# A fused attention, recurrence and mixture-of-experts kernel: the drain of its second phase in another written order, with a second buffer for the expert output

## The reference, cut to what matters

```python
x = x + _layernorm(attention(_layernorm(x)))        # 16 heads
x = x + _layernorm(fp8_gemm(_layernorm(x)))
x = x + _layernorm(hawk_block(_layernorm(x)))       # conv, gates, scan, gated MLP
x = x + _layernorm(mixture(_layernorm(x)))
```

## Time and profile before

| what | value |
|---|---|
| median of 3 runs | 1355.8 us |
| lowest, highest | 1354.93, 1356.39 us |
| profiled execution, its own time | 1354.26 us |
| its span from first to last instruction | 1352.5 us |
| mean granted TensorE clock | 0.957 |
| busy: PE, DVE, ACT, POOL | 1199.3 (89%), 1119.7 (83%), 974.4 (72%), 808.0 (60%) us |

### The profile page before, as it was taken

One profiled execution on the slowest core, in us unless ns is written; L12 is line 12 of the kernel. 1 busy time (PEld: TensorE's weight loads), 2 busy tenths in 40 slices (PEclk: granted clock), 3 DMA queues, 4 the chain that ended last, 5 costly groups with the idle time before them and its releaser, 6 DMA issues.

```text
span 1352.5 us, 26168 instructions
## 1 busy us (share of the span) xinstructions
PE 1199.3 (89%) x8688; PEld 497.3 (37%) x8688; DVE 1119.7 (83%) x2357; ACT 974.4 (72%) x1780; POOL 808.0 (60%) x1091
## 2 busy tenths in 40 slices
PE   1789999999999999999999999977979999999863
PEld 0223233333332333333333332333545555655442
DVE  2867999999999999999999899856658878878756
ACT  1267877887888787788788787777758687787640
POOL 6304447467466466466566545536878888888752
PEclk8589999999999999999999998999989999999985
DMA  1131011011011011011011010000000000000000
GB/s 50 52 88 43 27 45 42 28 44 41 29 44 39 31 43 40 31 43 39 32 43 33 29 36 12 2 1 1 1 8 9 9 16 8 9 17 9 16 9 24
DMA packets 52517, 37.87 MB, mean 28 GB/s; under 512 B 8864, under 2 KB 51744, under 8 KB 52384
## 3 DMA queue, kind: packets, MB, share of 16 engines
q1 hardware_dynamic: 52384, 36.22, 8.4%
HBM read 6.31 MB, written 4.19 MB: 8 GB/s over the span
## 4 chain that ended last, share of the span: by engine, by line
PE 34%; DVE 26%; issue 15%; POOL 11%; ACT 10%; SPq 4%; DMA 0%; ACTq 0%; POOLq 0%; DVEq 0%
PE bank L201 10%; PE bank L182 9%; DVE neg_max L493 9%; PE bank_pair L169 4%; PE bank L228 3%; SPq L641 3%; PE bank L210 3%; DVE probs L1172 2%; PE bank L235 2%; ACT probs L381 2%; DVE y_q L472 1%; ACT probs L1024 1%; POOL x_all L1491 1%; DVE probs L1348 1%; DVE probs L1344 1%
## 5 line engine op out<-in xcount | busy, mean ns | idle before, releaser
L381 ACT ACTIVATE probs<-bank 128x512 f32<-128x512 f32 x1024 | 569.4, 599 | 165.6 <-PE bank L182 163.1
L493 DVE TENSOR_REDUCE neg_max<-bank_pair 128x2 f32<-128x1024 f32 x512 | 610.3, 1214 | 88.4 <-PE bank_pair L169 86.2
L182 PE MATMUL bank<-q_stack,k_stack 50*128 50x512 bf16 x1024 | 352.3, 388 | 31.3 <-ACT probs L381 22.9
L201 PE MATMUL bank<-probs,v_pad 128*32 128x256 f32 x4096 | 331.9, 394 | 0.4 <-issue 0.2
L169 PE MATMUL bank_pair<-k_stack,q_stack 48*128 48x512 bf16 x1024 | 292.3, 395 | 33.5 <-DMA k_stack<-k_parts 18.0
L182 PEld LDWEIGHTS bank<-q_stack,k_stack 50*128 50x128 bf16 x1024 | 79.3, 93 | 275.6 <-ACT probs L381 234.2
L201 PEld LDWEIGHTS bank<-probs,v_pad 128*32 128x32 f32 x4096 | 83.0, 108 | 166.8 <-issue 160.3
L794 PE MATMUL bank_pair<-probs,w_gates 128*128 128x512 f32 x256 | 118.7, 607 | 5.8 <-DVE probs L1641 2.9
L567 POOL TENSOR_SCALAR tiny<-mv_b 128x4 f32<-128x4 f32 x16 | 4.0, 250 | 146.9 <-DVE mv_b L52 146.9
L522 POOL TENSOR_TENSOR q_rest<-q_rest,q_parts 128x512 f32<-128x512 f32 x16 | 20.2, 1260 | 119.7 <-ACT q_rest L325 119.7
L169 PEld LDWEIGHTS bank_pair<-k_stack,q_stack 48*128 48x128 bf16 x1024 | 53.9, 94 | 58.7 <-DVE neg_max L493 37.0
(11 more groups left out here) (249 smaller groups left out, 2250.2 us busy)
## 6 DMA issues: line engine op xcount, KB each, us to landing
q_stack<-q_parts SPq DMA_DIRECT2D x384, 32.0 KB
k_stack<-k_parts SPq DMA_DIRECT2D x384, 32.0 KB
x_all<-in_z_dram SPq DMA_DIRECT2D x16, 256.0 KB, 3.0
out_dram<-x_all SPq DMA_DIRECT2D x16, 256.0 KB, 2.3
q_stack<-max_rows SPq DMA_DIRECT2D x64, 8.0 KB
w_gates<-in_w_gates_dram SPq DMA_DIRECT2D x1, 512.0 KB, 3.8
w_in<-in_w_in_dram SPq DMA_DIRECT2D x1, 256.0 KB, 2.9
w_grow<-in_w_grow_dram SPq DMA_DIRECT2D x1, 256.0 KB, 4.0
```

Of the source, the lines that this page charges most:

```text
L182: nc.tensor.matmul(st_ps[h][:, :], k_stack[par][rows, p, c * P:(c + 1) * P], q_stack[par][rows, p, :], start=True, stop=True).then_inc(s[" ...
L201: mm = nc.tensor.matmul(acc[32 * g:32 * g + 32, cols], v_pad[bpar][:, kc, 4 * a + g, :], probs[:, at + g, cols], start=(t == 0 and kc == 0 ...
L381: nc.scalar.activation(probs[:, 4 * (n % RING) + g, :], st_ps[g % 2][:, :], ACT.Exp, scale=SCALE)\
L493: nc.vector.tensor_reduce(neg_max[j // 4][:, c, j % 4, :], score_ps[c % 2][:, :, :], AX_X, ALU.max, negate=True).then_inc(s["max_read"], 1)
```

## The change

In the drain only. PE: `gate_in(NB)` ahead of `cumulated(NB)`. ACT: `decay(NB)` ahead of `route_exps(NB)`. DVE: `routed_out(NB+1)` moves behind `ranks(NB+2)`, and `norm_x3(NB+2)` from behind `exps_inv(NB+2)` to ahead of `ranks(NB+2)`; the last batch's counts are neither summed nor added; its two instructions for the largest logit go ahead of the bias sum, and its mean and variance behind `exps_inv`. POOL: `root_x3(NB+2)` ahead of `routed_root(NB+1)`. The expert output of iteration NB+2 is written to `acc_y`, with statistics of its own. In the loop the written instructions are the same as before.

```diff
@@ tensor, drain
             forget(NB)
+            gate_in(NB)
             cumulated(NB)
-            gate_in(NB)
             wout(NB)
@@ scalar, drain
+            decay(NB)
             route_exps(NB)
-            decay(NB)
             square(NB)
@@ vector
+        def y_of(i):
+            return (acc_y, "y_odd") if i == NB + 2 else (y, "y")
+        def largest(i):
...
+        def below_largest(i):
...
+        def stats_y(i):
+            if live(i, -4):
+                aggregate(y_of(i)[1], "y", i - 4)
         def routed(i):
...
+                y, which = y_of(i)
                 wait(dve, s["y_ps"], b + 1)
+                if i > NB + 2:
+                    largest(i)
+                    below_largest(i)
                 if i > NB + 1:
-                    wait(dve, s["x4_ready"], b)
+                    wait(dve, s["x4_ready"], b - 1)
                 else:
                     wait(dve, s["yc_ready"], b)
                 TT(y..., bank_y..., consts["b_expert"]..., ALU.add).then_inc(s["y_ready"], 1)
+                if i <= NB + 2:
+                    largest(i)
                 wait(dve, s["y_ready"], b + 1)
-                raw("y", "y", chunk(y))
...
+                raw(which, "y", chunk(y))
+                if i <= NB + 2:
+                    below_largest(i)
+                    stats_y(i)
@@ place_sum
-                wait(dve, s["count_step"], 2 * b + 1)
-                TT(counts[:, :], counts[:, :], counted[:, :], ALU.add).then_inc(s["count_step"], 1)
+                if b < NB - 1:
+                    wait(dve, s["count_step"], 2 * b + 1)
+                    TT(counts[:, :], counts[:, :], counted[:, :], ALU.add).then_inc(s["count_step"], 1)
@@ vector, drain
             norm_t(NB + 2)
-            routed_out(NB + 1)
             raw_x3(NB + 2)
             stats_x3(NB + 2)
             routed(NB + 2)
+            norm_x3(NB + 2)
             ranks(NB + 2)
+            routed_out(NB + 1)
             exps_sum(NB + 2)
             exps_inv(NB + 2)
-            norm_x3(NB + 2)
             counts_of(NB + 2)
...
             exps_inv(NB + 3)
-            counts_of(NB + 3)
+            stats_y(NB + 3)
             place(NB + 3)
@@ pool, drain
             x3_sum(NB + 2)
+            root_x3(NB + 2)
             routed_root(NB + 1)
             routed_sum(NB + 1)
-            root_x3(NB + 2)
             routed_root(NB + 2)
```

More of the change, by code:

```diff
@@ L705, in hawk_moe_phase @@
     xc_pad = padded[:, 0:T + TAPS - 1]
-    stats = {n: (sb(f"bn_{n}", [P, C, 6]), sb(f"mv_{n}", [P, C, 2])) for n in ("t", "x3", "y")}
+    stats = {n: (sb(f"bn_{n}", [P, C, 6]), sb(f"mv_{n}", [P, C, 2])) for n in ("t", "x3", "y", "y_odd")}
     h_sum = sb("h_sum", [P, C])
@@ L1185, in taps @@
                     conv[par][:, 1, :], ALU.mult, ALU.add).then_inc(q, 1)
+        def y_of(i):
+            return (acc_y, "y_odd") if i == NB + 2 else (y, "y")
+        def largest(i):
+            b, q = i - 4, s["top_step"]
+            wait(dve, s["logits_ps"], b + 1)
+            nc.vector.tensor_reduce(top[:, 0, :], log_ps.rearrange("p (c e) -> p c e", e=E), AX_X, ALU.max)\
+                .then_inc(q, 1)
+        def below_largest(i):
+            b, q = i - 4, s["top_step"]
+            wait(dve, q, 2 * b + 1)
+            wait(dve, s["route_step"], 5 * b)
+            wait(dve, s["exps_ready"], b)
+            TT(shifted[:, :, :], log_ps.rearrange("p (c e) -> p c e", e=E),
+               top[:, 0, :].unsqueeze(2).to_broadcast([P, C, E]), ALU.subtract).then_inc(q, 1)
+        def stats_y(i):
+            if live(i, -4):
+                aggregate(y_of(i)[1], "y", i - 4)
         def routed(i):
@@ L1196, in routed @@
                    consts["b_expert"][:, :].unsqueeze(1).to_broadcast([P, C, D]), ALU.add).then_inc(s["y_ready"], 1)
[L1197 to L1200, removed]
+                if i <= NB + 2:
+                    largest(i)
                 wait(dve, s["y_ready"], b + 1)
-                raw("y", "y", chunk(y))
[L1203 to L1208, removed]
+                raw(which, "y", chunk(y))
+                if i <= NB + 2:
+                    below_largest(i)
+                    stats_y(i)
         def routed_out(i):
             b = i - 4
+            y, which = y_of(i)
             wait(dve, s["rs_y_step"], 5 * (b + 1))
-            scaled(y, chunk(y), stats["y"][1], rs["y"][:, 2, :], s["yn_part"])
+            scaled(y, chunk(y), stats[which][1], rs["y"][:, 2, :], s["yn_part"])
             wait(dve, s["yn_part"], C * (i - NB))
@@ L1508, in routed_root @@
                 wait_apart(gp, s["stat_y"], C * (b + 1), past_wait)
-                TT(top[:, 5, :], top[:, 4, :], stats["y"][1][:, :, 1], ALU.mult).then_inc(q, 1)
+                var = stats["y_odd" if i == NB + 2 else "y"][1][:, :, 1]
+                TT(top[:, 5, :], top[:, 4, :], var, ALU.mult).then_inc(q, 1)
                 wait_apart(gp, q, at + 2, past_wait)
```

## The result

| | before | changed |
|---|---|---|
| median, us (10 runs each) | 1354.66 | 1347.29 |
| lowest to highest | 1350.48 to 1356.63 | 1344.52 to 1350.92 |
| ratio of the two, 95% interval | | 0.9946 [0.9933, 0.9959] |
| span of the profiled execution | 1352.5 | 1343.6 |

The changed kernel is 7.4 us (0.54%) faster by medians, 5.5 to 9.1 by the interval. The forecast was 1349.9 with a range of 1346.5 to 1352.8.

The account below looks back on a forecast made before the run. The prediction took the drain to be bound by late gate_in(NB) on PE and norm_x3(NB+2) on DVE. Gains 2.2 + 3.2 = 5.4 from a mean of 1355.35 gave 1349.9, range 1346.5 to 1352.8.

Parts of the forecast that it names:

- the two places: In the drain's chain: gate_in(NB) on PE at 1280.92, 5.06 us, and norm_x3(NB+2) on DVE at 1335.34.
- The gates on PE and ACT: gate_in(NB) follows forget without pause at full clock; ACT reaches its tanh pair L1057 at 1281.37, 4.64 earlier.
- Exclusion between VectorE and GpSimd: Around the scans of iteration NB, wide instructions exclude each other, leaving 2.2 of 4.64; L1477 starts at 1292.0.
- The clock: On PE from wout(NB+1) onward: chain as before, only 2.2 earlier, so no gain or loss from clock in the sum.
- rival (c): PE from 1301.0 to 1322.3: a fifth to a quarter at half speed, losing about 3, giving 1352.9; chance 0.14.
- part 1: Last gates: gate_in(NB) ahead of cumulated(NB) on PE, decay(NB) ahead of route_exps(NB) on ACT; gain 2.2 us.
- The last batches: End of drain: norm_x3(NB+2) and routed_out(NB+1) reordered, second buffer; last logits at 1335.1 instead of 1338.30, gain 3.2.
- Inner order and counts of the last batch: Last batch on DVE: 5.21 from y stays within 0.2, and the counts left out gain nothing.
- ACT's half of part 1: On ACT, decay(NB) no longer waits for shifted and starts at 1277.69 instead of 1279.14; no separate gain given.
- rival (a): DVE and POOL collide not at all or more cheaply: gains 6.6 to 7.8, 1347.6 at the far end; chance 0.22.
- its own signs: Things to see in the profile, among them the last batch's bias sum L1195 near 1336.7 with both gains.
- Rival (d): PE's clock stays at 1.2 GHz through 1301.0 to 1322.3: slower than before, 1357.8; chance 0.05.

Follow-up runs that it names:

- Small_pool: Changed kernel with GpSimd's three wide instructions of iteration NB cut from 512 to 4 elements a partition; 1348.61 us, ratio 0.9951.
- no_act: Changed kernel with ACT's old order, route_exps(NB) ahead of decay(NB); 1348.33 us over 12 runs, ratio 0.9948.
- pe_only: Kernel before with only PE's gate_in(NB) moved ahead of cumulated(NB), ACT as before; 1351.28 us, ratio 0.9973.
- p1_only: Kernel before with only gate_in(NB) ahead of cumulated(NB) on PE and decay(NB) ahead of route_exps(NB) on ACT; 1353.26 us, ratio 0.9985.
- pool_late: Changed kernel with GpSimd's mixture work of iteration NB moved later, whole, behind norm_h(NB) to x3_sum(NB) and further steps; 1351.27 us, ratio 0.9968.
- after_again: Changed kernel measured a second time, no edit, against the kernel before; 1348.84 us against 1354.74, ratio 0.9959.
- pool_fit: Changed kernel with GpSimd's mixture work of iteration NB moved into gaps away from VectorE's L1172 groups; 1345.52 us (7 runs), ratio 0.9942.
- p2_only: Changed kernel with both PE's and ACT's reorderings of the gates undone; 1349.42 us, ratio 0.9963.
- one_buffer: Changed kernel with a single buffer y, routed_out(NB+1) ahead of routed(NB+2), root_x3(NB+2) behind routed_sum(NB+1); one run, 1349.68 us.

## Why the prediction was right, point by point

The forecast named the two places, the new wait in each and the sign of every term of its sum. Against the profile of the changed kernel:

- **The gates on PE and ACT.** Forecast 4.64 earlier for the tanh pair; measured 8.71 - 3.98 = 4.73. No pause on PE, and ACT sets the moment and not PE, if only by 0.08: both as said.
- **Exclusion between VectorE and GpSimd.** Forecast as the reason why only 2.2 of 4.64 arrive; measured 2.69, since the collisions cost 2.04 and not 2.4. The order of events is the one that was played through: L1541 waits for L1325, L1479 for L1367, the first scan for L1479, L1495 for the first scan, L1497 for the second. Small_pool shows that it is GpSimd's wide work: without it 2.06 comes back. The rule of the Trainium skill (page "SBUF — State Buffer", section "SBUF: two separate sides") gave the right reading for the wide instructions; by a sum without it the drain would have been 2 us shorter than it was. For GpSimd's small power instruction the whole-instruction lock does not fit the trace (last section), and there the measurement decides; the forecast had taken its length from the rows.
- **The clock.** This term was missing from the sum. The forecast took `wout(NB+1)` and the growth products as unchanged; in the changed kernel's profile the third stretch is 0.92 shorter (11.07 against 11.99), because the clock returned sooner (0.56 in `wout(NB+1)` and 0.40 in the growth products, less 0.04 elsewhere). The clock stood in the range and in rival (c), with the sign the other way. And `gate_in` after its pause, taken as 5.06, is 6.6 in another profile, so part 1's gain was undersized for some executions.
- **The last batches.** Forecast 3.2, measured 23.02 - 19.58 = 3.44. The logits are released by `placed` as said. Of the two edits that bring them forward, `norm_x3`'s place is worth 2.56, the second buffer with `routed_out`'s place 1.6 (not additive: each alone leaves the transposes late). `routed_out(NB+2)` and the last y did tie, with no wait added.
- **Inner order and counts of the last batch, GpSimd's root.** Forecast nothing, 0.06 and 0.12 measured. ACT's half of part 1 was not priced by itself. Up to `norm_h(NB)` it costs 0.34 (no_act) to 0.53 (pe_only against p1_only), since it moves VectorE into GpSimd's way; over the whole drain the profiles do not settle its sign.
- **The sum.** 2.69 + 0.92 + 3.44 = 7.05 in the drain, against 5.4. The mis-sized terms are the clock (0.9), the collisions (0.4), the gates (0.1) and the last batches (0.2). Of the 2.6 between 1349.9 and 1347.29, another 0.7 is the level of the kernel before, 1354.66 over ten runs and not 1355.35.
- **Luck, and the scatter.** The measured 1347.29 lies nearer to rival (a)'s 1347.6 than to the forecast, and yet (a), the rival without collisions, did not happen: the scans took 3.28, and L1500 (L1477 before) came 14.18 into the drain, where (a) needed 12.3. The time was inside the range by a margin that was put there for another mechanism and for scatter; the timeline, and not the time, shows that the forecast's mechanism is the one. The scatter itself was taken as 0.16% from four values; ten runs of the kernel before spread over 0.45%. By the second set of runs, 0.41%, the forecast of 0.40% looks exact, which is chance as well. Of its own signs, one missed: the last bias sum starts at 1333.59 + 1.84 = 1335.43 in the old profile's times, 1.3 ahead of the 1336.7 forecast.

Rival (d), the clock at 1.2 GHz through 1301 to 1322, did not show in any of the 14 profiles: the fourth stretch, which covers most of it, is 19.99 to 20.01 in all but pool_late.

Open stays how much of the gain by time is the clock. In the drain it is 0.92 of 7.05 in the first profile and 0.55 of 6.68 in after_again. The third stretch is 11.32 us on average in the seven profiles in which GpSimd is held up (10.20 in the second stretch), and 11.95 in the six, pool_fit aside (its centring adds 0.67 there), in which the stretch ahead of it is short (8.14 to 8.34). Taking GpSimd's delay away thus seems to bring the low clock into `wout`, and to give back a part of the gain, but with a spread of up to 1.25 within a group that is a tendency and not a price. Nor does PE's idle time ahead of it settle it: the kernel before, p2_only and pool_fit all had 5.73 us of it, and their `wout` took 3.75, 3.14 and 3.05.

## What to carry to other kernels

When an instruction off the critical path is moved into another engine's idle time, ask who used that idle time: the gates came 4.7 us earlier and 2.0 of it went to wide GpSimd work that had been hidden behind the wait. Where a step has two conditions, price both (`placed` and the transposes here); following one alone gives the wrong worth for an edit, as my expectation for one_buffer showed. And where single runs spread by more than the effect, cut the profile at fixed events: stretches that repeat to 0.1 us tell apart what medians of ten runs can't. Keep the stretches in which the clock changes apart, and take no price from one profile of those.

## What the runs showed of the hardware beyond that

- VectorE's tensor-scalar instruction with a single wide on-chip f32 input takes turns with wide GpSimd instructions as well (four in 2.66 and 2.05 instead of 1.11, pool_late), not only those with two inputs.
- A short VectorE instruction waits as well. In the kernel before, L1223 of iteration NB took 0.89 beside GpSimd's L1456, and 0.16 with nothing beside it (1334.52). So some 0.7 of the pause of 2.96 ahead of `cumulated` was itself such a wait, since `chosen` stands behind L1223:

```profile
1279.22 0.89 DVE L1223 SCALAR_TENSOR_TENSOR ranked<-shifted,rev 128x32 f32<-128x32 f32 x1
```

```profile
1278.79 1.27 POOL L1456 TENSOR_TENSOR x_all<-x_all,zn 128x512 f32<-128x512 f32 x1
```

- GpSimd's power on 128x4 is different from its wide instructions: it waits for its turn, but holds VectorE up hardly at all. In the kernel before, L1474 took 1.83 and the two scans beside it 2.34; two scans at 916.07, with GpSimd idle, took 2.34 as well.
- After a pause of 2.9 us the clock stayed at 1.2 GHz for about 3 us of solid matmuls in one profile and for about 6 in another (5.21 and 6.62 for the same eight); `wout(NB+1)`, the same 16 matmuls, took 3.02 to 3.76 over the profiles.
